# Attention and feed-forward in one kernel: both score rows of a step transposed by one instruction and moved through DRAM as one

## The reference

```
x: [2048, 256];  16 heads of 128;  W_K, W_Q, W_V: [16, 128, 256];  W_O: [256, 2048]
xn  = layernorm(x)
k, q, v = xn W_K^T, xn W_Q^T, xn W_V^T              # per head, [2048, 128]
s   = q k^T, causal (masked entries -1e10)
a   = softmax(s / sqrt(128))                        # per query row
att = sum over heads of (a v) W_O^T
ffn = (fwht(silu(xn W1^T) * (xn W3^T))) W2^T        # hidden width 1024
out = x + att + ffn
```

## Time and profile before

| | |
|---|---|
| median of 3 runs | 1453.58 us |
| profiled execution | 1462.46 us, span 1460.6 us, mean TensorE clock 0.978 |
| busy: TensorE | 1354.9 us (93%) |
| busy: VectorE / ScalarE / GpSimd | 955.0 / 930.6 / 996.5 us |
| DMA packets | 278459, 335.14 MB, 229 GB/s over the span; 251280 of them under 2 KB, 62736 under 512 B |
| block transposes (L767) | 256, 322.0 us |
| casts to pt_hi (L555) / splits to pt_lo (L378) | 384, 283.3 us / 384, 661.4 us |

### The profile page before, as it was taken

One profiled execution on the slowest core, in us unless ns is written; L12 is line 12 of the kernel. 1 busy time (PEld: TensorE's weight loads), 2 busy tenths in 40 slices (PEclk: granted clock), 3 DMA queues, 4 the chain that ended last, 5 costly groups with the idle time before them and its releaser, 6 DMA issues.

```text
span 1460.6 us, 26628 instructions
## 1 busy us (share of the span) xinstructions
PE 1354.9 (93%) x8104; PEld 1195.5 (82%) x8104; DVE 955.0 (65%) x2133; ACT 930.6 (64%) x1879; POOL 996.5 (68%) x660
## 2 busy tenths in 40 slices
PE   3999999969999999999999999999999999999986
PEld 2878888758888888888888888888888888888876
DVE  6643300277777777776777777777777777776760
ACT  3312334456767777777777777777777777777772
POOL 4420000066979797979797979797979797888785
PEclk8899999989999999999999999999999999999997
DMA  4100056588798988887988798988888888888884
GB/s 146 69 1 0 0 144 195 158 241 280 226 289 260 284 265 278 267 270 252 284 251 283 247 285 267 288 268 280 258 280 281 264 276 259 277 267 276 253 259 151
DMA packets 278459, 335.14 MB, mean 229 GB/s; under 512 B 62736, under 2 KB 251280, under 8 KB 273808
## 3 DMA queue, kind: packets, MB, share of 16 engines
q1 hardware_dynamic: 278416, 334.65, 73.1%
HBM read 173.08 MB, written 161.48 MB: 229 GB/s over the span
## 4 chain that ended last, share of the span: by engine, by line
POOL 40%; issue 27%; PE 21%; DVE 5%; DMA 2%; ACT 2%; SPq 2%; POOLq 1%; DVEq 0%; ACTq 0%
POOL pt_lo L378 26%; POOL acc L369 9%; PE ps L825 7%; PE ps L826 7%; PE ps L827 7%; POOL v_lo L383 2%; SPq L276 1%; DVE raw L767 1%; ACT raw L546 1%; DVE had L757 1%; POOL wqk_hi L354 1%; POOL wqk_lo L356 1%; DMA raw<-w3t 1%; DMA pt_lo<-scratch 1%; DMA scratch<-raw 1%
## 5 line engine op out<-in xcount | busy, mean ns | idle before, releaser
L378 POOL TENSOR_TENSOR pt_lo<-pt_lo,pt_hi 128x640 fp32r<-128x640 f32 (+11 forms) x384 | 661.4, 1754 | 168.2 <-ACT pt_hi L555 167.3
L546 ACT ACTIVATE raw<-ps,had 128x1024 f32<-128x1024 f32 (+7 forms) x384 | 330.3, 868 | 265.1 <-DVE had L760 251.7
L767 DVE STREAM_TRANSPOSE raw<-raw 128x2048 f32<-128x2048 f32 (+15 forms) x256 | 322.0, 1291 | 75.2 <-ACT raw L546 72.9
L825 PE MATMUL ps<-pt_hi,v_hi 128*128 128x256 f32 (+1 forms) x1152 | 327.2, 284 | 17.7 <-POOL pt_lo L378 16.2
L826 PE MATMUL ps<-pt_lo,v_hi 128*128 128x256 f32 (+1 forms) x1152 | 331.9, 288 | 0.0
L827 PE MATMUL ps<-pt_hi,v_lo 128*128 128x256 f32 (+1 forms) x1152 | 330.3, 287 | 0.0
L555 ACT CAST pt_hi<-pt_lo 128x640 fp32r<-128x640 f32 (+11 forms) x384 | 283.3, 817 | 28.1 <-DMA pt_lo<-scratch 27.8
L757 DVE TENSOR_REDUCE had<-ps 128x1 f32<-128x1024 f32 (+1 forms) x256 | 237.8, 949 | 54.6 <-PE ps L827 54.3
L825 PE MATMUL ps<-k_hi,q_hi 128*128 128x512 f32 (+3 forms) x640 | 237.7, 371 | 7.5 <-ACT raw L546 7.5
L825 PEld LDWEIGHTS ps<-pt_hi,v_hi 128*128 128x128 f32 x1152 | 222.4, 193 | 24.9 <-issue 15.8
L827 PE MATMUL ps<-k_hi,q_lo 128*128 128x512 f32 (+3 forms) x640 | 234.6, 367 | 0.0
(11 more groups left out here) (102 smaller groups left out, 2249.7 us busy)
## 6 DMA issues: line engine op xcount, KB each, us to landing
all_values<-raw SPq DMA_DIRECT2D x16, 1024.0 KB, 5.1
v_next<-all_values SPq DMA_DIRECT2D x16, 1024.0 KB, 5.3
scratch<-raw SPq DMA_DIRECT2D x64, 256.0 KB, 5.8
pt_lo<-scratch SPq DMA_DIRECT2D x16, 1024.0 KB, 5.3
scratch<-raw SPq DMA_DIRECT2D x64, 240.0 KB, 5.0
pt_lo<-scratch SPq DMA_DIRECT2D x16, 960.0 KB, 6.1
scratch<-raw SPq DMA_DIRECT2D x64, 224.0 KB, 5.3
pt_lo<-scratch SPq DMA_DIRECT2D x16, 896.0 KB, 4.8
```

The costliest lines, as they stand in the source:

```text
L378: pool.tensor_tensor(lo, lo.bitcast(F32), hi.bitcast(F32), ALU.subtract).then_inc(pt_lo_done, 1)
L546: act.activation(to[:, first // P:(first + n) // P], ps[:, a * BANK:a * BANK + n].rearrange("p (i g k) -> p i g k", g=4, k=BLK), ACT.Exp, ...
L767: dve.transpose(v, v).then_inc(blocked, 1)
L825: pe.matmul(dst, a[0], b[0], start=start, stop=False, skip_group_check=True)
```

## The change

Both rows of a step now lie side by side in one stretch of 18 tiles of `raw`, written by the same three exponentials. In an even step only 17 of them are filled, and tile 17 is moved out but not back. One block transpose covers all 18 tiles. One scratch tensor for each step takes four transfers out, with runs of 18 * 32 elements (2304 bytes), and gives one transfer back, in runs of 17 or 18 tiles' blocks. `stored` and `moved` are one semaphore each. The casts and splits have two pieces a step, each two query blocks wide over all 17 or 18 tiles, in place of three. The weighted sums wait for both pieces of a pair's second step. In the small chunks the tiles of the two query rows lie the same way as before, and in the big ones they are swapped, which `output` undoes. The tile that only one of the two rows sees is read from the other half there.

The diff, cut to its core:

```diff
-        RAW = 17 * P
+        RAW = 18 * P
...
-        scratch = [nc.dram_tensor(f"scratch{j}", [P, (j + 1) * P], F32).ap() for j in range(TILES)]
+        scratch = [nc.dram_tensor(f"scratch{s}", [P, RAW], F32).ap() for s in range(STEPS)]
+        def first_tile(s, small):
+            return TILES - 2 * (s // 2) if small else 0
+        def tiles_of(s):
+            return 17 + s % 2
+        def raw_step(s):
+            return raw[:, (s % 2) * RAW:(s % 2 + 1) * RAW]
+        def pt_step(t, s, first=0, last=4):
+            b = (s % 2) * 4
+            return pt_pair(t, s // 2)[:, b + first:b + last, 0:tiles_of(s), :]
...
-            def send(h, s, small):
-                sp.wait_ge(blocked, 2 * (STEPS * h + s) + small + 1)
-                wait(sp, stored[small], 64 * (STEPS * h + s))
+            def send(h, s):
+                sp.wait_ge(blocked, STEPS * h + s + 1)
+                wait(sp, stored, 64 * (STEPS * h + s))
+                to = scratch[s].rearrange("(g k) (a x) -> a k g x", a=4, g=4)
                 for a in range(4):
-                    sp.dma_start(to[a], raw_row(s, small)[...]).then_inc(stored[small], 16)
+                    sp.dma_start(to[a], raw_step(s)[...]).then_inc(stored, 16)
-            def bring(h, s, small):
+            def bring(h, s):
                 if s % 2 == 0:
-                    wait(sp, z_product, (z_count(h - 1, 5), z_count(h - 1, 7),
-                                         z_count(h, 1 if small else 0), z_count(h, 3 if small else 2))[m])
+                    wait(sp, z_product, (z_count(h - 1, 5), z_count(h - 1, 7), z_count(h, 1), z_count(h, 3))[m])
-                sp.wait_ge(stored[small], 64 * (STEPS * h + s + 1))
+                sp.wait_ge(stored, 64 * (STEPS * h + s + 1))
+                sp.dma_start(to, back[:, :, 0:tiles_of(s) * BLK]).then_inc(moved, 16)
...
+            pool.memset(raw[:, 2 * HEADS_D:2 * RAW], 0.0).then_inc(mask_ready, 1)
...
             def p_to_hi(h, s, n):
-                a, b = ((0, 2), (2, 4), (0, 4))[n]
-                act.wait_ge(moved[n == 2], 16 * (STEPS * h + s + 1))
+                act.wait_ge(moved, 16 * (STEPS * h + s + 1))
+                hi, lo = (pt_step(t, s, 2 * n, 2 * n + 2) for t in (pt_hi, pt_lo))
...
-            def transpose_blocks(h, s, small):
-                dve.wait_ge(exped, piece_count(h, s, 2 if small else 1))
-                v = raw_row(s, small).rearrange("p (b k) -> p b k", k=BLK)
+            def transpose_blocks(h, s):
+                dve.wait_ge(exped, exp_count(h, s, 2))
+                v = raw_step(s).rearrange("p (b k) -> p b k", k=BLK)
                 dve.transpose(v, v).then_inc(blocked, 1)
...
                     if not over:
-                        transpose_blocks(h, s, 0)
+                        transpose_blocks(h, s)
                     if s == 7 and more:
                         kq_to_lo(h, ("K", 1))
-                    if not over:
-                        transpose_blocks(h, s, 1)
...
-                    pe.wait_ge(pt_lo_done, piece_count(h, 2 * (z // 2) + 1, 2 if z % 2 else 1))
+                    pe.wait_ge(pt_lo_done, piece_count(h, 2 * (z // 2) + 1, 1))
-                    lo = 4 if i == 2 * c + 1 else 0
+                    lo, hi = (0, 8) if i <= 2 * c else (4, 8) if z % 2 else (0, 4)
```

More of the change, by code:

```diff
@@ L309, in _ @@
                     if hh >= 0:
-                        bring(hh, ss, 0)
-                        bring(hh, ss, 1)
-                    send(h, s, 0)
-                    send(h, s, 1)
+                        bring(hh, ss)
+                    send(h, s)
                     if s == 5 and h + 1 < HEADS:
                         bring_v(h + 1)
-            bring(HEADS - 1, STEPS - 1, 0)
-            bring(HEADS - 1, STEPS - 1, 1)
+            bring(HEADS - 1, STEPS - 1)
             for z in range(CHUNKS):
@@ L372, in p_to_lo @@
             def p_to_lo(h, s, n):
-                j = row_of(s, n == 2)
-                a, b = ((0, 2), (2, 4), (0, 4))[n]
-                lo, hi = pt_row(pt_lo, j, a, b), pt_row(pt_hi, j, a, b)
+                lo, hi = (pt_step(t, s, 2 * n, 2 * n + 2) for t in (pt_lo, pt_hi))
                 pool.wait_ge(pt_hi_done, piece_count(h, s, n))
@@ L405, in period @@
                     if not (first and s < 2) and not (over and s >= 2):
-                        for n in range(3):
+                        for n in range(2):
                             p_to_lo(hh, ss, n)
@@ L539, in exponential @@
                 if e == 0:
-                    for i in range(2):
-                        wait(act, stored[i], 64 * (STEPS * h + s - 1))
-                        if isinstance(h, int) and h == 0 and s < 2:
+                    wait(act, stored, 64 * (STEPS * h + s - 1))
+                    if isinstance(h, int) and h == 0 and s < 2:
+                        for i in range(2):
                             act.wait_ge(v_stored[i], 16 * TILES // 2)
-                to = raw_row(s, small).rearrange("p (g i k) -> p i g k", g=4, k=BLK)
-                act.activation(to[:, first // P:(first + n) // P],
+                to = raw_step(s).rearrange("p (g i k) -> p i g k", g=4, k=BLK)
+                at = first_tile(s, small) + first // P
+                act.activation(to[:, at:at + n // P],
                                ps[:, a * BANK:a * BANK + n].rearrange("p (i g k) -> p i g k", g=4, k=BLK), ACT.Exp,
@@ L569, in output @@
                     j = 2 * c + t
-                    ins = act.activation(share[:, z % 2, t, :], ring_bank(("O", z))[:, t * D:(t + 1) * D], ACT.Copy,
+                    at = t if z % 2 else 1 - t
+                    ins = act.activation(share[:, z % 2, t, :], ring_bank(("O", z))[:, at * D:(at + 1) * D], ACT.Copy,
                                          scale=row_rcp[:, j:j + 1])
@@ L810, in period @@
                         kq_to_lo(h, (("Q", 3), ("Q", 0), ("K", 2))[s - 5])
-            dve.wait_ge(mask_ready, 2)
+            dve.wait_ge(mask_ready, 3)
             for item in KQ_ITEMS[2:]:
@@ L961, in scores @@
                     if pos == 0 or exp_of(ss, pos) != exp_of(ss, pos - 1):
-                        wait(pe, exped, piece_count(hh, ss, exp_of(ss, pos)) if not first_step(h, s) else 0)
+                        wait(pe, exped, exp_count(hh, ss, exp_of(ss, pos)) if not first_step(h, s) else 0)
                     if s == 0 and pos < 3:
@@ L989, in weighted_sum @@
                     i = tiles[n]
-                    lo = 4 if i == 2 * c + 1 else 0
+                    lo, hi = (0, 8) if i <= 2 * c else (4, 8) if z % 2 else (0, 4)
                     v = [t[:, i * P:(i + 1) * P] for t in (v_hi, v_lo)]
-                    p = [pt_chunk(t, c)[:, lo:8, i, :] for t in (pt_hi, pt_lo)]
-                    ins = mm3(bank(Z, lo * BLK, CHUNK_Q), v, p, n == 0, n == len(tiles) - 1)
+                    p = [pt_chunk(t, c)[:, lo:hi, i, :] for t in (pt_hi, pt_lo)]
+                    ins = mm3(bank(Z, lo * BLK, hi * BLK), v, p, n == 0, n == len(tiles) - 1)
                 if end == len(tiles):
```

39 lines of the change are left out of this document (15 added, 24 removed).

## The result

The changed kernel takes 1558.14 us, the median of 6 runs (1552.21 to 1561.98); the kernel before took 1454.19 beside it (6 runs, 1452.34 to 1457.56). The ratio is 1.0723, 95% interval 1.0704 to 1.0742: slower by 104 us. The forecast was 1514 and its range ended at 1546. The direction was right, the size was not. The transfer chain did become a bound, which the second rival had at 1543 us and a chance of 0.14.

The account below looks back on a forecast made before the run. It took TensorE's order as the bound, with SyncE's transfer chain almost equally long. Terms 29.6 + 18.2 + 12.8 = 60.6 us on 1462.5 gave 1523.1 profiled, less 8.9: 1514 us; own range 1495 to 1530, 8-in-10 range 1474 to 1546.

Parts of the forecast that it names:

- the second rival: Transfer chain overtakes TensorE and bounds, with gaps of 2.3 us: 77.2 us a head, about 1543 us; chance 0.14.
- K1 behind the transposes: Step 7: k_lo of block K1 comes after the single transpose, delaying TensorE's output product 1.97 us in 15 heads, 29.6 us.
- The later maxima: Steps 1 and 3: later, longer transposes and casts delay VectorE's maxima and TensorE by 1.21 us a head, 18.2 us.
- The wait for both pieces: Step 4: the big weighted sum needs both new GpSimd pieces, 0.8 us later, 16 times, 12.8 us.
- The chain: SyncE's loads and stores through scratch: 74.4 us a head, just under TensorE's 75.6, so adding nothing of its own.
- The gap: Between last store and next load, emptied by the single semaphore: 1.9 us in seven steps a head, 2.3 at the upper end.
- The rule weighed there: Skill page: a transfer's fixed part is mostly the write receipt's wait, worst to HBM; speaks against joining rows behind one semaphore.
- What was said to show it: k_lo's wait 9 to about 35 us, z_lo's 45 to 60 or more, pt_lo's 16 to 28; DMA share about 0.80.
- three signs of being wrong: k_lo's wait under 1 us a head, loads following in under 8.9 us, or waits for the first scores growing instead.

Follow-up runs that it names:

- late_transposes: The kernel before, with both block transposes of a step waiting for the third exponential and k_lo of block K1 made ahead of both: 1466.36 us, ratio 1.0082.
- k1_three: The changed kernel with k_lo of block K1 made ahead of the transpose and casts and splits in the old three pieces, load left whole: 1522.48 us, ratio 1.0483.
- sum_waits_all: The kernel before, with the big weighted sums waiting for all three pieces of their last step, not the first two: 1483.59 us, ratio 1.0214.
- join_stores: The kernel before, with only the big row's load waiting for the stores of both rows, not of the big row alone: 1548.12 us, ratio 1.0675.
- k1_last: The kernel before, with only k_lo of block K1 in step 7 moved behind both transposes: 1465.76 us, ratio 1.0083.
- the halves: A load cut in two, each half waiting for two stores: 1449.33 us in the kernel before; 1475.03 in the changed kernel with K1 ahead and three pieces.
- half_loads: The changed kernel with a step's one load cut into two, each half waiting only for the two stores that hold its query blocks: 1551.90 us, ratio 1.0704.
- before_halves: The kernel before, with the big row's load in two halves, each waiting for two of its four stores: 1449.33 us, ratio 0.9982.
- k1_first: The changed kernel with k_lo of block K1 made ahead of the single transpose in step 7: 1528.23 us, ratio 1.0531.

## Why the prediction was wrong

**K1 behind the transposes: right in place, wrong in reach.** Forecast 1.97 us a time, measured 2.09, and 31.4 in the run where 29.6 were worked out. By itself in the kernel before it costs 12 us, since a stall there is 18.7 and a third is given back; in the changed kernel it is worth 28, and there the load of step 6's rows waits for the sum behind it (33.0 us of z_product with it, 2.6 without).

**The later maxima: right within bounds.** Forecast 18.2 us of a possible 6 to 24; 12 measured by itself, in late_transposes, which leaves out the 0.14 of the casts.

**The wait for both pieces: under-sized.** The forecast took 0.8 us at step 4 only, 12.8 us. Alone it costs 31, in 48 waits. The rows of the other pairs' sums had not been read: they start without a wait before (15 waits in the whole run, one a head), and their slack was taken as enough without looking.

Added up, these three measured alone make 12 + 12 + 31 = 55 us, beside the 60.6 of the forecast's sum. That the sum is near is luck: 29.6 was more than twice too much for K1 and 12.8 less than half of what the pieces cost. And single effects do not add here, as shown below.

**The chain: the step that failed.** It reads "it lies just under TensorE's 71.6 + 3.98 = 75.6. It adds nothing of its own at my values." The chain's own length came near, 74.4 against 75.2 in k1_three, with two errors that offset each other: the gap was 0.4 us too short, and the rate of a head too low (328 GB/s for 256 / 0.76 = 337). Three things in the conclusion were wrong. First, it compared two loops and took the longer, as if they ran free of each other. They don't: TensorE waits for `pt_lo`, which the chain fills, and the chain waits for the sums that empty it. Each stall of either is passed on, so the head takes 77.0 us, more than either forecast length. Second, the diff had joined the wait for the sums as well: the load, whole now, waits for z_count(h, 1) and (h, 3), the small sums, where the big row's load waited for 0 and 2. That line stood in the diff and was given no cost. In the changed kernel the load waits 33.0 us there. What the joining of this wait costs by itself was not tested: the wait is 2.6 us with K1 in time and 3.9 with the old pieces, so it costs only when TensorE's sums are late; and sum_waits_all, which does not join it, has 37.3. Third, the lateness of a load does not appear as a wait of the chain alone; join_stores shows it on ScalarE and then in z_lo, 98 us for one wait.

**The gap.** Taken as 1.9 us with 2.3 as the upper end; it is 2.3 [the window 778.5 to 780.8]. The second rival used that end and had 77.2 us a head; 77.0 came. That is near in part by luck: the rival had the chain alone at 77.2, where the chain alone took 75.2, and the rest is the coupling.

**The rule weighed there.** The Trainium skill, DMA: Bandwidth & Descriptors, section Anatomy of one DMA, puts the fixed part of a transfer mostly on the wait for the write's receipt, and I said that it spoke against joining the rows. The section is on transfers that GpSimd issues, and these go out on SyncE's queue. The empty 2.3 us fit the rule; no run here shows which part of them is a receipt. The page's section Bandwidth, by which larger transfers should win, did not decide this kernel: 42% fewer packets came with 7% more time.

**What was said to show it.** The weight loads' wait for k_lo: about 35 us, and 36.6 came. Transposes: 128 of 2.58, and so it is. DMA share: 0.80, and 0.78 came between 400 and 1300 us. The chain's step: 9.3 to 9.5, but 9.63. pt_lo: 28, but 71.1. z_lo: to rise to 60, but it fell to 27.4, as it does in sum_waits_all too. My reading is that a sum that waits for pt_lo leaves VectorE and ScalarE time to catch up; that was not tested. None of the three signs of being wrong that it named appeared; they watched K1, a chain that gets shorter and the first scores, and nothing watched the load's wait for the sums.

**What cannot be added.** The single effects must not be added. join_stores, sum_waits_all, k1_last and late_transposes cost 98 + 31 + 12 + 12 = 153 us alone and the change costs 104 with all of them. How the 104 divide has no one answer: the halves win 3 us first or 50 last.

## What to carry to other kernels

When transfers are joined, their waits are joined, and the wait can cost more than the transfer saves: look at what now moves in the gap between the last store and the first load, and if nothing does, keep one semaphore for each part that can be used alone. Where two loops are within a few per cent of each other and each waits for the other's room, the longer of the two is only a lower bound (77.0 us a head here, against 75.2 and 75.6); every wait in the diff that links them needs its own row. An experiment that cuts one of several joined waits can show nothing (half_loads) though it is worth 50 us once the others are gone.

## What the runs showed of the hardware

**The clock after a stall.** TensorE's products cost 20 us more in the changed kernel, with the same shapes, at a mean granted clock of 0.965 for 0.978. After the idle 2.09 us before 817.18 the granted clock was 0.83 in the next window and 0.57 in the one behind, most of it spent at the lower of the two levels, 1.2 of 2.4 GHz, though TensorE was busy in nearly all of both. The products of 512 columns show it, in the timeline of the changed kernel:

```profile
820.91 0.63 PE L834 MATMUL ps<-k_hi,q_lo 128*128 128x512 f32 x1
821.33 0.63 PE L832 MATMUL ps<-k_hi,q_hi 128*128 128x512 f32 x1
...
822.37 0.39 PE L832 MATMUL ps<-k_hi,q_hi 128*128 128x512 f32 x1
822.60 0.39 PE L833 MATMUL ps<-k_lo,q_hi 128*128 128x512 f32 x1
```

The first two start 0.42 us apart, and from 822.37 on 0.23. In this head TensorE's busy time is 70.36 us against the 68.24 of the earlier trace rows. This stall so costs more than its length. join_stores is also busy for longer (1377.8 us, clock 0.966), and before_halves for less (1345.5, 0.985). Which stalls do it is not shown: k1_last has 15 stalls of up to 1.3 us at the same place and is busy 1348.0 us (0.982), and k1_first, without K1's stalls, is still busy 1373.7 (0.966). The forecast had no term for it.

**Long runs.** With runs of 2304 bytes the DMA engines moved 354 GB/s at a share of 0.94, against 315 at 0.96 in the earlier trace rows. Over a whole head it is 256 / 0.76 = 337 against 271 / 0.87 = 311. No run changes the length of the runs alone. The faster rate did not pay for the empty gaps: over the whole run q1, the queue that carries these transfers, was busier before (73.1%) than after (67.4%).
